# A mixture of experts that gathers only the rows each expert was chosen for, and a state space kernel built by doubling, against the dense form

## What is computed

```
scores = sigmoid(x @ gate_weight.T)          # 32 experts in 4 groups
tw     = scores of the 6 best experts of the 2 best groups, normalised, * 0.2
routed = sum over the 6 chosen e of tw[e] * (silu(x @ w_gate[e]) * (x @ w_up[e])) @ w_down[e]
shared = silu(x @ s_gate) * (x @ s_up) @ s_down
anchor = the same with one of 16 small experts (width 64), that of the best expert's pair
x      = x + routed + shared + 0.1 * anchor
# by-product, needed first in the state space stage:
K[d, l] = 2 * Re( sum over 64 n of dC[d, n] * exp(dtA[d, n] * l) ),  l = 0..1023
```

## Time and profile before

| | us |
|---|---|
| median of the runs | 3484.33 |
| profiled execution | 3483.8 (span 3482.0) |
| first stage | 0 to 166.9 |
| MoE stage | 166.9 to 1188.3 |
| of it, before the turns begin | 166.9 to 244 |
| later stages | 1188.3 to 3482.0 |

### The profile page before, as it was taken

How to read it: one execution, slowest core, us unless ns; L and a number is a source line. 1 busy time by engine, 2 the same in 40 slices (tenths; PEclk the granted TensorE clock), 3 DMA queues, 4 the chain that set the end, 5 groups by cost and what they waited for, 6 DMA issues and landing times. The chain is left out here.

```text
span 3482.0 us, 32507 instructions
## 1 busy us (share of the span) xinstructions
PE 2875.0 (83%) x11790; PEld 1862.0 (53%) x11790; DVE 1877.6 (54%) x5012; ACT 659.9 (19%) x1098; POOL 628.5 (18%) x586
## 2 busy tenths in 40 slices
PE   6859999998999889989899999997746855865759
PEld 4635555555555555557567777676512422543436
DVE  4647555555111224441578777679497664357441
ACT  2212332333111111110211111111010001224111
POOL 0004545554222100000012122112011230001000
PEclk8969999999999958997899899898755777987579
DMA  2033112211211100031000000000200002010000
GB/s 62 20 134 113 38 43 51 46 42 34 56 52 52 29 30 0 1 118 34 1 1 1 1 1 1 1 1 1 82 1 1 0 0 70 0 52 1 0 3 21
DMA packets 69392, 104.06 MB, mean 30 GB/s; under 512 B 15429, under 2 KB 41353, under 8 KB 68289
## 3 DMA queue, kind: packets, MB, share of 16 engines
q1 hardware_dynamic: 69233, 101.99, 10.0%
HBM read 94.65 MB, written 3.54 MB: 28 GB/s over the span
## 5 line engine op out<-in xcount | busy, mean ns | idle before, releaser
L131 PE MATMUL PS<-mem 128*128 128x256 f32 (+12 forms) x11038 | 2744.6, 412 | 233.3 <-DVE mem L1995 56.8
L131 PEld LDWEIGHTS PS<-mem 128*128 128x128 f32 (+9 forms) x11038 | 1771.5, 191 | 1174.5 <-issue 802.7
L1508 POOL TENSOR_TENSOR mem<-mem 128x512 f16<-128x512 f16 x128 | 155.7, 1216 | 1112.5 <-DVE mem L1476 1112.5
L1122 POOL TENSOR_TENSOR mem<-mem 128x512 f32<-128x512 f32 x160 | 221.1, 1382 | 648.4 <-DVE mem L1095 638.0
L1095 DVE TENSOR_TENSOR mem<-PS,mem 128x512 f32<-128x512 f32 x160 | 109.9, 687 | 386.4 <-PE PS L131 307.1
L1483 DVE TENSOR_TENSOR mem<-mem,PS 128x512 f32<-128x512 f32 x128 | 156.4, 1222 | 167.7 <-PE PS L131 157.1
L1035 ACT ACTIVATE mem<-PS 128x512 f32<-128x512 f32 x164 | 95.4, 596 | 511.0 <-PE PS L131 510.6
L188 PE MATMUL PS<-mem 128*128 128x128 f32 x128 | 53.9, 422 | 153.1 <-DVE mem L254 81.8
L670 DVE SCALAR_TENSOR_TENSOR mem<-mem 128x512 f32<-128x512 f32 (+1 forms) x212 | 157.4, 742 | 7.4
L417 DVE TENSOR_REDUCE mem<-PS 128x4 f32<-128x308 f32 (+1 forms) x112 | 49.8, 444 | 203.5 <-PE PS L131 203.5
L1475 DVE TENSOR_TENSOR mem<-mem 128x2048 f16<-128x2048 f16 x128 | 155.7, 1216 | 0.0
(11 more groups left out here) (196 smaller groups left out, 1857.7 us busy)
## 6 DMA issues: line engine op xcount, KB each, us to landing
mem<-scr_cw SPq DMA_DIRECT2D x128, 256.0 KB, 3.2
mem<-scr_cw SPq DMA_DIRECT2D x64, 128.0 KB, 3.0
mem<-in_downT SPq DMA_DIRECT2D x1, 4096.0 KB, 16.2
mem<-in_up_embed SPq DMA_DIRECT2D x1, 4096.0 KB, 26.9
mem<-in_moe_g SPq DMA_DIRECT2D x9, 384.0 KB, 9.0
mem<-in_moe_u SPq DMA_DIRECT2D x9, 384.0 KB, 9.5
mem<-in_moe_d SPq DMA_DIRECT2D x9, 384.0 KB, 10.0
mem<-in_x SPq DMA_DIRECT2D x4, 512.0 KB
```

The source lines that it names most:

```text
L131: return e.matmul(out, lhsT, rhs, start=start, stop=stop, skip_group_check=True)
L1122: p(e.tensor_tensor(AC[:, u, :], UU[:, u, :], SG[:, u, :], ALU.mult), s["ac"])
L1508: p(e.tensor_tensor(R[:, n % 2, :, :], R[:, n % 2, :, :], bc(w, 1, (128, 32, 16)), ALU.mult), s["weighted"])
```

## The change

**Weights and table early.** ACT gets 14 DMA issues at the head of its program in the first stage (ExpertWeights.prefetch), behind a wait for that stage's inputs: ten that clear a DRAM table (158 tiles x 128 rows x 280 numbers, 22.6 MB, rows of 1120 bytes), and four that load weights (12.4 MB). The last 12 experts' weights (4.7 MB) are loaded by SP later.

**Routing.** Each token's row is x (256 numbers), its six expert numbers, six weights and seven destinations. DVE chooses, counts and ranks the tokens of each expert (prefix sums, two products with a triangular matrix on PE), and so gives each (token, choice) a slot in the table; each expert's slots are rounded up to whole tiles of 128: at most 2048*6/128 + 31 = 127 tiles, and 31 for the anchors. All 158 are always computed. POOL scatters the rows into the table with 96 indirect DMAs of 128 rows, and 16 for the anchors.

**Shared expert.** Computed first, densely, 4 groups of 512 tokens.

**State space kernel.** No longer in the background: between the routing and the tile loop, DVE alone prepares one exponential per channel and state and its powers by squaring, then doubles a table five times for each of 16 chunks of 8 channels in each half; PE makes 32 small products per chunk; two stores for four chunks. The MoE loop does not begin until it is stored.

**Tile loop.** 158 tiles: SP loads table rows in batches of 4, PE transposes (2), makes 2 products of 256 columns with weights whose address comes from a register loaded per 16 tiles, ACT takes silu, DVE gates with the row's weight, PE transposes once, DVE copies, PE makes one product of 256 columns, ACT copies, POOL scatters 128 rows of 1 KB to a second DRAM table (14.7 MB in all). Then SP loads that table in 8 parts and DVE sums the seven rows of each token into x.

Semaphores are now handed out from a pool and reused by stages; this adds no instruction.

```diff
+    def prefetch(self, e):                      # ACT, first stage, ahead of ln_sqrt
+        e.wait_ge(*self.s["zeroed"](1))
+        flat = self.table.rearrange("(p i) w -> p i w", p=128)
+        n = NTILE // 10 + 1
+        for i in range(10):
+            a, b = i * n, min(i * n + n, NTILE)
+            e.dma_start(flat[:, a:b, :], bc(self.zero, 1, (128, b - a, WIDE))).then_inc(c, 16)
+            if i == 2:
+                e.dma_start(self.WS, d["moe_s"]).then_inc(w, 16)
+                e.dma_start(self.WE[:, mid:], d["moe_e"][:, mid:]).then_inc(w, 16)
...
     def act(self, e):                            # xattn_heads
+        if ew:
+            e.wait_ge(*k.g0["x_in"](16 * 7))
+            e.wait_ge(*s["xa_w"](NW))
+            ew.prefetch(e)
         ln_sqrt(k, e, s, 0, range(NT))
...
+    def chunk_dve(self, e, v, c):                # state space kernel, 16 times
+        v(e.tensor_copy(P[:, :, :, 0], self.first[:, :, c, :]))
+        for n in range(5):
+            m = 1 << n
+            v(e.tensor_tensor(Tr, P[:, :, :, 0:m], wr, ALU.mult))
+            v(e.tensor_tensor(Ti, P[:, :, :, 0:m], wi, ALU.mult))
+            v(e.tensor_tensor(P[:, 0, :, m:2 * m], Tr[:, 0], Ti[:, 1], ALU.subtract))
+            v(e.tensor_tensor(P[:, 1, :, m:2 * m], Tr[:, 1], Ti[:, 0], ALU.add), ...)
...
+        for i in range(NTILE + 3):               # PE, the tile loop
+            if i < NTILE: turn(i)
+            if 1 <= i <= NTILE: up(i - 1)
+            if 2 <= i <= NTILE + 1: turn_h(i - 2)
+            if i >= 3: down(i - 3)
...
     def pool(self, e, p):
+        for t in range(NT):
+            for i in range(TOPK):
+                e.indirect_dma_start(ew.table, bass.IndirectOffsetOnAxis(ap=POS[:, i, t:t + 1], axis=0), xe[:, t, :],
+                                     None).then_inc(s["sent"].h, 16)
...
+            e.wait_ge(*s["t_yc"](n + 1))
+            e.indirect_dma_start(ew.parts, bass.IndirectOffsetOnAxis(ap=IDX[:, n:n + 1], axis=0), Y[:, n % NY, :], None,
+                                 bounds_check=T * (TOPK + 1) - 1, oob_is_err=False).then_inc(s[f"y_out{n % NY}"].h, 16)
```

More of the change, by code:

```diff
@@ L279, in wait_ht, with start @@
         e.wait_ge(*either(s["ht_a"], s["ht_v"], t))
-def start(k):
+def start(k, ew):
     d = k.d
-    s = k.g0 = k.sigs(x_in=16 * 8, ones=1)
+    s = k.g0 = k.kept(x_in=16 * 7, ones=1)
     def sp(e):
@@ L607 @@
 SH = 0.9999995
-def step(gen, n):
-    for _ in range(n):
-        next(gen, None)
 class StateKernel:
[L618 to L642, removed]
+    NCH = 128 // JC
@@ new lines, in chunk_act @@
+    def chunk_act(self, e, c, bank):
+        s = self.s
+        q = c % 4
+        e.wait_ge(*s["s4_prod"](c + 1))
+        if q == 0 and c:
+            e.wait_ge(*s["s4_out"](32 * (c // 4)))
+        for h in range(2):
+            last = e.activation(self.Kt[:, :, h, q * JC:(q + 1) * JC].rearrange("p a d -> p d a"),
+                                self.k.PS[0:32, bank + 2 * h, 0:JC * 32].rearrange("p (d a) -> p d a", d=JC),
+                                ACT.Copy)
+        last.then_inc(s["s4_copied"].h, 1)
@@ new lines, in pe @@
+        for g in range(5):
+            if g < 4:
+                shared_up(g)
+            if g:
+                shared_down(g - 1)
+        e.wait_ge(*s["sh_g"](4))
+        e.wait_ge(*s["sh_u"](4))
+        e.wait_ge(*s["chosen"](1))
+        for h in range(2):
+            mm(e, PS[:, 4 + h, 0:384], tri, sel[:, 8 * h:8 * h + 8, :].rearrange("p t e -> p (t e)"), True, True)
+            last = mm(e, PS[:, 2 * h, 0:384], k.ones, sel[:, 8 * h:8 * h + 8, :].rearrange("p t e -> p (t e)"), True, True)
@@ new lines, in pe @@
+        last.then_inc(s["ranks"].h, 1)
+        e.wait_ge(*s["emap"](1))
+        for i in range(2):
+            last = mm(e, PS[:, 3, i * 128:(i + 1) * 128], eb[:, i, :], k.ident, True, True)
+        last.then_inc(s["etab"].h, 1)
+        e.wait_ge(*s["rows_r"](1))
+        e.wait_ge(*s["pos"](1))
+        for c in range(sk.NCH):
+            sk.chunk_pe(e, c, c % 2)
+        e.wait_ge(*sk.s["s4_copied"](sk.NCH))
+        e.wait_ge(*s["sh_yc"](8))
+        e.wait_ge(*ew.s["w_late"](16))
+        regs = [e.alloc_register(f"expert{i}") for i in range(32)]
@@ L1043, in dve, with choose @@
+    def choose(e, v):
         v(e.tensor_tensor(sb_, sc, bc(gb, 1, (128, NT, 32)), ALU.add))
@@ L1126, in moe @@
-    k.kernel_out = kernel_.s["s4_out"]
+        v(e.tensor_scalar(nt, nt, -MAGIC, None, ALU.add))
+        a_, b_ = nt, inc[0]
+        for m in (1, 2, 4, 8):
+            v.prev()
+            v(e.tensor_copy(b_[:, :, 0:m], a_[:, :, 0:m]))
+            v(e.tensor_tensor(b_[:, :, m:], a_[:, :, m:], a_[:, :, 0:16 - m], ALU.add))
+            a_, b_ = b_, (inc[1] if b_ is inc[0] else inc[0])
+        v.prev()
+        v(e.tensor_scalar(a_[:, 1, :], a_[:, 1, :], a_[:, 0, 15:16], None, ALU.add))
+        ends = a_.rearrange("p a b -> p (a b)")
@@ new lines, in place @@
+        for i, m in enumerate((NE, NA)):
+            v(e.tensor_scalar(ecol[:, i:i + 1], ecol[:, i:i + 1], m - 1.0, None, ALU.min))
+        v.prev()
+        for i in range(2):
+            v(e.tensor_scalar(eb[:, i, :], k.ones, ecol[:, i:i + 1], None, ALU.mult), s["emap"] if i else None)
+        for i, h in enumerate(halves):
+            v(e.tensor_tensor(dst[:, h, :], src[:, h, :], total[i], ALU.subtract))
+        v.prev()
+        for i, h in enumerate(halves):
+            v(e.tensor_tensor(src[:, h, :], dst[:, h, :], rank[i], ALU.add))
```

942 lines of the change are left out of this document (547 added, 395 removed).

## The result

The changed kernel takes **3141.5 us** (median of 4 runs, 3098.8 to 3162.8) against 3477.8 (also of 4) of the kernel before, run beside it. That is 0.903; two of the four runs, 3157.4 (the profiled one) and 3162.8, count as slow, being over 1.5% above the fastest, and without them the ratio is 0.894 (95% interval 0.883 to 0.904). Forecast were 3180 and a range of 3070 to 3420. A second set of four runs gave 3133.7, ratio 0.895 (0.893 to 0.897). The profiled execution took 3157.4 us with a span of 3155.5; all rows of after are from it.

The account below looks back on a forecast made before the run. The prediction took PE's work to bound the MoE stage, 1021 of 3482 us. From 3483.8 it took 380 off for that stage and added 75 for the first: 3179, or 3180 us, range 3070 to 3420.

Parts of the forecast that it names:

- The forecast case: Whole kernel: MoE stage 380 us shorter, first stage 75 longer, likeliest 3180 us; 3120 to 3240 was given 36%.
- ACT held, +75: First stage: ACT is held issuing the clears until the queue has room, so the whole stage moves by 75 us.
- rival 3: First stage: ACT is not held, so the kernel takes 3105 us; chance 12%.
- Lead and slots: MoE stage's start: choice 19 us, placing 21 plus a 3 us wait; slots known at 262, before the first stage's shift.
- State space kernel: Between routing and tile loop: DMAs 6 us, preparation 36, 16 chunks 109 on DVE; tile loop begins at 439 before the shift.
- Scatters: Beside the state space kernel: POOL's 96 indirect DMAs at 1.4 us each, 134 us, hidden up to 1.8 us apiece.
- Tile loop, the step that failed: 158 tiles: PE's own work 239.5 us, 282 with handoffs, plus 33 for address computations, together 315 us.
- factor 1.176 for handoffs: Tile loop: handoffs between engines lengthen PE's work as in the first stage, 239.5 to 282 us.
- 33 us for address computations: Tile loop: 474 address computations in PE's queue at 0.07 us each.
- Tail: Sum of the seven rows: reading 14.7 MB takes 39.7 us, plus 2.1 and DVE's last two tiles 4.9, 47 us.
- Later stages, 0: Stages after the MoE stage: they keep their work, so their time changes by 0.
- Rival 5: State space kernel: DVE and POOL hold each other off, 109 and 134 us exclude each other, kernel 3313 us; chance 9%.

Follow-up runs that it names:

- the two runs above: Changed kernel with all fourteen prefetch issues moved from ACT to SP: 3030.3 us, ratio 0.867; and with only the ten clears moved to SP: 3087.3 us.
- the doubled product: Changed kernel with the last product (256 columns) of each of the 158 tiles issued twice: 3239.4 us in the first execution, 3205.1 in the second set.

## Why the prediction came out right, and where it was off

The forecast case came true: none of the rivals, and the three large terms have the causes that were given for them (less work for PE, ACT held, later stages untouched). Their sizes were less exact. The MoE stage became 440 us shorter where 380 were forecast, the first stage 76 longer (75), and the later stages 37 longer in the profiled execution (0).

- **ACT held, +75**: measured 76. The reasoning by the earlier trace rows (an issuing engine is released when what it issued last fits into the queue) held within 2 us, and rival 3 is excluded by the trace and by the two runs above. That the transfers went at 370 GB/s was the other half: from 21 to 95 us the DMA engines moved 364 GB/s, 26.9 MB, where the prediction had 27.1. (What was left to the end, two clears and the anchors' weights, is 8.5 MB by its sizes and not 8.0, a slip of 1 us.) The Trainium skill, page "Perfetto Trace Analysis", section "DMA Instruction — HWDGE (DVE, Sync)", describes such an issue as lasting until all its descriptors are generated, with the DMA engines starting earlier where they don't all fit in the buffer. The trace is in line with it: 0.45 us for a load in long rows, 21.9 for three clears.
- **Lead and slots**: first scatter predicted at 262 + 75 = 337, measured 336.8. Two errors of a few us cancelled: the strided reduction of 3072 elements took 5.5 us instead of 3.4, other operations less.
- **State space kernel**: loads 8, preparation 35 (36 predicted), chunks 96 (109). PE's 64 small products take 1.94 us (5.6 predicted: 30 ns each at half the clock, where the price taken was 88). From the last chunk to the first tile it took 20 us (24 predicted). The loop began at 495.8, predicted 439 + 75 = 514: 18 early.
- **Scatters**: 1.31 us for 1.4, and hidden: done at 462.9, with DVE's chunks until 475.5.
- **Tile loop, the step that failed**: 315 predicted, 261 measured. Of its factors, 239.5 us of PE's own work was right for the full tiles (1.60 predicted, 1.63 measured); the anchor tiles take almost as long as the full ones, 1.55 for 1.17, 12 us too few. The factor 1.176 for handoffs, taken from the first stage, and the 33 us for address computations were both nothing that the trace or the doubled product shows. The factor was too large even for the first stage: the earlier trace rows has PE busy 9.09 of 10 us there, so no more than 9% of that tile is waiting. And the ratio was carried over without asking whether the order was the same: in the first stage PE's weight loads for the transposes wait 0.86 us in each tile for DVE, here the next tile's transposes stand between a tile's two products. That this order is the reason is argued from the traces, and no run changed it.
- **Tail**: 47 predicted, 63.6 measured. The price of an element in a contiguous operation was used for a strided reduction. With it the reading of the table (39.7 us) and DVE's 16 tiles (39) would have been about even, and the prediction let the reading decide; measured, DVE starts 7 us after the loads are issued and decides from there on.
- **Later stages, 0**: right for the change; the profiled execution drew +37.
- **Sum**: -18 - 54 + 16.5 - 3 (drain and rounding) + 37 = -21.5 on 3179, which is the 3157.4 of the profiled execution. The two largest misses, 54 and 37, had opposite signs, so the forecast was nearer than its parts; that is luck. The median of the runs lies 16 us below the profiled execution, 38 below the forecast.

Rival 5 (DVE and POOL exclude each other in the state space kernel) did not happen in the kernel's own executions: DVE's two-input operations take 0.28 us for 128 elements and 0.69 for 512 beside the scatters, the 0.69 of the earlier trace rows. By the Trainium skill, page "SBUF — State Buffer", section "Who interferes with whom", a DVE instruction with two SBUF inputs contends with a GpSimd instruction that reads SBUF, and not with one that only writes it. The rows agree with that if an indirect DMA doesn't read there; it takes its row numbers from the on-chip memory (POS), and no row shows how. The disturbance costs the same place 91 us, where rival 5 priced 134, but by another way: operations are not longer, their increments are late.

## What to carry to other kernels

Ahead of many short rows, ask which engine issues the DMA and what stands behind it there: moving fourteen issues from ACT to SP is worth 76 us here, and the work is the same. The loop whose next tile is transposed between this tile's products ran at PE's columns; do not carry a waiting factor over from a loop with another order. Judge an edit by its stage when another stage moves with the clock by more than the edit is worth.

## What had not been expected of the hardware

- An indirect DMA of 128 rows costs POOL 0.96 us + 0.30, whether its rows are 1 KB of results or 1120 bytes of table, and with nothing else in the way they follow each other every 1.27 to 1.29 us; DVE's operations beside it are not longer.
- A reduction over a stride of 256 elements costs DVE 3.16 us for 1792 elements and 5.54 for 3072, 1.7 to 1.8 ns an element, against 1.04 for contiguous ones.
- Matmuls of 64 x 32 by 64 x 32 follow each other every 30 ns at a clock of 0.50 (64 in 1.94 us).
- In some executions DVE's semaphore increments go one per 1.4 us, beginning some 23 us after POOL's first scatter and ending some 14 us after its last. Cause open.
